# Squares of y: eight transposes a head replaced by 32x32 block turns and one small product

## What is computed

```
xn = layernorm(x)
q, k = rmsnorm(xn @ Wq), rmsnorm(xn @ Wk)          # per head of 128
attn = softmax(q k^T / sqrt(128) - slope * distance, causal)
y    = attn @ v                                    # 1024 x 128 per head
y    = y * rsqrt(mean(y*y over the 128 channels) + 1e-5) * subln_w
out  = x + concat(y) @ Wproj + ffn(xn)
```

## Time and profile before

| | |
|---|---|
| median of 3 runs | 545.61 us (545.49 to 545.79) |
| the profiled execution's own time | 543.86 us |
| its span, first to last instruction | 541.7 us |
| PE busy | 520.0 us (96%) |
| DVE, ACT, POOL busy | 414.7, 391.8, 334.3 us |
| granted TensorE clock | 1.00 of full speed throughout |

### The profile page before, as it was taken

How to read it: one execution, slowest core, us unless ns; L and a number is a source line. 1 busy time by engine, 2 the same in 40 slices (tenths; PEclk the granted TensorE clock), 3 DMA queues, 4 the chain that set the end, 5 groups by cost and what they waited for, 6 DMA issues and landing times.

```text
span 541.7 us, 11888 instructions
## 1 busy us (share of the span) xinstructions
PE 520.0 (96%) x3430; PEld 479.1 (88%) x3430; DVE 414.7 (77%) x1031; ACT 391.8 (72%) x887; POOL 334.3 (62%) x430
## 2 busy tenths in 40 slices
PE   7869899999999999999999999999999999999985
PEld 3868799999999999999999999999999999999874
DVE  5768778787788877877887877888778778868775
ACT  2668687686867778687777868778786876878662
POOL 4659575774758647684767748587476856647121
PEclk9999999999999999999999999999999999999999
DMA  5200101001010100101010010101001000000002
GB/s 150 69 1 2 40 0 41 2 1 41 2 39 0 39 0 0 39 0 39 0 39 0 0 39 0 39 0 31 8 0 39 0 10 0 11 1 1 2 1 79
DMA packets 18614, 10.83 MB, mean 20 GB/s; under 512 B 2208, under 2 KB 18592, under 8 KB 18592
## 3 DMA queue, kind: packets, MB, share of 16 engines
q1 hardware_dynamic: 17600, 10.49, 6.7%
q10 hardware_dynamic: 992, 0.07, 0.1%
HBM read 9.51 MB, written 1.05 MB: 19 GB/s over the span
## 4 chain that ended last, share of the span: by engine, by line
PE 87%; DVE 6%; ACT 3%; issue 2%; DMA 1%; POOL 1%; POOLq 0%; DVEq 0%; SPq 0%
PE pT_ps L564 11%; PE qkv_ps L479 10%; PE qkv_ps L481 8%; PE qkv_ps L480 8%; PE yT_ps L481 7%; PE yT_ps L480 7%; PE yT_ps L479 7%; PE score_big L479 5%; PE score_big L480 4%; PE score_big L481 4%; PE misc L540 3%; PE score_small L481 2%; PE score_small L480 2%; PE score_small L479 2%; ACT stage L743 2%
## 5 line engine op out<-in xcount | busy, mean ns | idle before, releaser
L934 DVE TENSOR_TENSOR pT_lo<-pT_ps,pT_hi 128x384 fp32r<-128x384 f32 (+1 forms) x192 | 101.0, 554 | 41.4 <-ACT pT_hi L771 41.2
L743 ACT ACTIVATE stage<-qkv_ps 128x384 f32<-128x384 f32 x119 | 58.7, 493 | 85.0 <-PE qkv_ps L481 84.5
L763 ACT ACTIVATE probs<-probs,neg_max 128x1024 f32<-128x1024 f32 (+7 forms) x128 | 98.5, 770 | 16.6 <-DVE neg_max L925 16.5
L771 ACT ACTIVATE pT_hi<-pT_ps 128x384 fp32r<-128x384 f32 (+1 forms) x192 | 86.3, 484 | 18.6 <-PE pT_ps L564 14.0
L432 POOL TENSOR_TENSOR y_r<-y_ms,minus_half 128x4 f32<-128x4 f32 x32 | 32.7, 1023 | 105.7 <-DVE y_ms L953 105.7
L479 PE MATMUL qkv_ps<-w_hi,xT_hi 128*128 128x384 f32 x242 | 87.2, 360 | 3.3 <-DVE xT_lo L994 0.7
L564 PE MATMUL pT_ps<-ident,probs 128*128 128x128 f32 x576 | 84.5, 274 | 4.2 <-ACT probs L763 3.5
L480 PE MATMUL qkv_ps<-w_lo,xT_hi 128*128 128x384 f32 x242 | 81.5, 337 | 0.0
L481 PE MATMUL qkv_ps<-w_hi,xT_lo 128*128 128x384 f32 x242 | 81.5, 337 | 0.0
L392 POOL TENSOR_TENSOR qk_r<-qk_ms,minus_half 128x4 f32<-128x4 f32 x64 | 65.5, 1024 | 20.9 <-DVE qk_ms L899 20.3
L564 PEld LDWEIGHTS pT_ps<-ident,probs 128*128 128x128 f32 x576 | 66.4, 140 | 9.2 <-ACT probs L763 4.4
(11 more groups left out here) (183 smaller groups left out, 1310.1 us busy)
## 6 DMA issues: line engine op xcount, KB each, us to landing
w_raw<-in_wq SPq DMA_DIRECT2D x16, 128.0 KB, 2.2
w_raw<-in_wk SPq DMA_DIRECT2D x16, 128.0 KB, 2.3
w_raw<-in_wv SPq DMA_DIRECT2D x16, 128.0 KB, 2.3
wp_raw<-in_wproj SPq DMA_DIRECT2D x16, 128.0 KB, 2.1
acc<-in_x SPq DMA_DIRECT2D x4, 256.0 KB, 4.8
out<-acc SPq DMA_DIRECT2D x8, 128.0 KB, 1.8
w<-in_ffn_w ACTq DMA_DIRECT2D x1, 64.0 KB, 5.2
q_col<-in_q_w ACTq DMA_DIRECT2D x1, 0.5 KB, 3.0
```

What stands on the lines that cost most here:

```text
L743: act.activation(stage_of(h, k // 2)[:, k % 2, :], qkv_bank(h, k)[:, 0:3 * D], ACT.Copy).then_inc(qkv_read, 1)
L763: act.activation(probs[:, s % 2, 0:(i + 1) * P], probs[:, s % 2, 0:(i + 1) * P], ACT.Exp, bias=neg_max[:, par, s:s + 1], scale=-1.0, accum ...
L771: act.activation(pT_hi[g][:, a:b, r * P:(r + 1) * P], pT_ps[(CHUNK0[s] + k) % 2][:, 0:(b - a) * P].rearrange("p (j t) -> p j t", t=P), ACT ...
L934: dve.tensor_tensor(pT_lo[g][:, a:b, r * P:(r + 1) * P], pT_ps[(CHUNK0[s] + k) % 2][:, 0:(b - a) * P].rearrange("p (j t) -> p j t", t=P), ...
```

## The change

The squares are taken on ACT straight from `yT_ps` (`square_y`, now in place of the copy to `y_raw`). DVE turns the 128x512 squares in blocks of 32x32 (`part_y`): after that a partition holds, for one token modulo 32, 32 channels of one quarter side by side, and a reduction over 32 gives `y_part`, 16 numbers per partition. Partition 32a+i then holds the sums over the channels of quarter a, for the tokens i of each block of 32. POOL splits `y_part` into hi and lo (`split_y`, two operations of 128x16), PE adds the four quarters by one product with the constant `quarters` (1/128 where the partitions agree modulo 32), 32 columns wide (`sum_y`). DVE masks with `in_quarter` which of four results belongs to the partition (`y_pick`) and reduces nine numbers per token tile, the eps term among them. `norm_y` and `add_out` stay. The two constants are made on DVE at the program's start.

Around it: `qkT0` moves from step 3 to step 4 and into the bank `yT`, so that `transpose_qk` 0 and 1 stand where one of them and a `turn_y` stood; ACT's `qk_hi` 0 and 1 both move, to the two sides of the last `copy_qkv` of step 4; DVE's mean of group 1 moves from step 5 to step 3; POOL's `split_y` of group 0 stands ahead of `split_w`.

```diff
-    MISC = ["ss0", "proj0a", "proj0b", "qkT0", "ss1", "qkT1", "qkT2", "qkT3", "proj1a", "proj1b"]
-    JOB_BANK = {"ss0": "qkv", "proj0b": "yT", "ss1": "yT", "qkT2": "qkv", "proj1a": "qkv"}
-    TAIL_BANK = {"ss0": "qkv", "proj0a": "small", "proj0b": None, "ss1": "big0", "proj1a": "qkv", "proj1b": "big1"}
+    MISC = ["proj0a", "proj0b", "qkT0", "qkT1", "qkT2", "qkT3", "proj1a", "proj1b"]
+    JOB_BANK = {"proj0b": "yT", "qkT0": "yT", "qkT2": "qkv", "proj1a": "qkv"}
...
+            def split_y(h, g):
+                pool.wait_ge(y_summed, 2 * h + g + 1)
+                past(pool, y_crossed, 2 * h + g)
+                pool.nop(nofuse=True)
+                part = y_part[:, :].rearrange("p (r c) -> p r c", c=4)
+                pool.tensor_copy(y_pair[:, :, 0, :], part).then_inc(y_part_hi, 1)
+                pool.wait_ge(y_part_hi, 2 * h + g + 1)
+                pool.nop(nofuse=True)
+                pool.tensor_tensor(y_pair[:, :, 1, :], part, y_pair[:, :, 0, :].bitcast(f32),
+                                   ALU.subtract).then_inc(y_paired, 1)
...
                 if tile is not None:
                     round_x(tile)
+                if not first:
+                    split_y(h - 1, 0)
...
                 if not (isinstance(h, int) and h + 2 >= H):
                     split_w(h + 2, par)
...
+                        if k == 0 and not first:
+                            split_y(h - 1, 1)
...
+                if job == "proj0a" and not tail:
+                    pe.wait_ge(y_picked, 2 * h - 1)
+                if job == "qkT1" or tail and bank == "qkv":
+                    past(pe, y_picked, 2 * h - 1 if tail else 2 * h)
...
-            def turn_y(h, g, now):
-                bank_free(now, f"ss{g}")
-                pe.wait_ge(y_copied, 2 * h + g + 1)
-                for r in range(4):
-                    last = pe.transpose(job_ps(h + 1, f"ss{g}")[:, r * P:(r + 1) * P], y_raw[:, g, r * P:(r + 1) * P],
-                                        ident[:, :])
-                last.then_inc(y_turned, 1)
+            def sum_y(h, g):
+                pe.wait_ge(y_paired, 2 * h + g + 1)
+                past(pe, y_picked, 2 * h + g)
+                if is_last(h) and g == 0:
+                    pe.wait_ge(misc_read, misc_done(h, "proj1a"))
+                elif is_last(h):
+                    pe.wait_ge(scores_masked, NT * H)
+                elif g == 0:
+                    pe.wait_ge(misc_read, misc_done(h, "qkT3" if isinstance(h, int) and h == 0 else "proj1b"))
+                else:
+                    pe.wait_ge(misc_read, misc_done(h + 1, "proj0a"))
+                if isinstance(h, int) and (h, g) == (0, 0):
+                    pe.wait_ge(w8T_read, 1)
+                pe.matmul(sum_ps(h, g), quarters[:, :], y_pair[:, :, :, :].rearrange("p r l c -> p (r l c)"),
+                          start=True, stop=True).then_inc(y_crossed, 1)
...
-                            turn_y(h - 1, 0, h)
                     if s == 1:
+                        if not first:
+                            sum_y(h - 1, 0)
...
-                        if s == 4 and not first:
-                            turn_y(h - 1, 1, h)
-                        elif not first:
+                        if s == 4 and not last:
+                            transpose_qk(h + 1, 1 - par, 0, h)
+                            transpose_qk(h + 1, 1 - par, 1, h)
+                        if s < 4 and not first:
                             if s == 3 and tile is not None:
                                 pe.wait_ge(ffn_added, tile + 1)
+                            if s == 3:
+                                sum_y(h - 1, 1)
                             project_out(h - 1, 1 - par, 0, s - 2, h)
                         if not last:
                             project(h + 1, 1 - par, 2 * s - 1)
-                    if s in (3, 4) and not last:
-                        transpose_qk(h + 1, 1 - par, s - 3, h)
...
-            turn_y(H - 1, 0, H)
             project_out(H - 1, 1, 0, 0, H)
+            sum_y(H - 1, 0)
             attend(H - 1, 1, 1, 0)
             attend(H - 1, 1, 1, 1)
             project_out(H - 1, 1, 0, 1, H)
-            turn_y(H - 1, 1, H)
+            sum_y(H - 1, 1)
...
-            def y_out(h, g):
+            def square_y(h, g):
                 act.wait_ge(yT_ready, 2 * h + g + 1)
-                act.activation(y_raw[:, g, :], yT_ps[:, :], ACT.Copy).then_inc(y_copied, 1)
+                past(act, y_turned, 2 * h + g - 1)
+                act.activation(y_sq[:, g, :], yT_ps[:, :], ACT.Square).then_inc(y_squared, 1)
+            def y_hi(h, g):
                 act.activation(yT_hi[:, g, :], yT_ps[:, :], ACT.Copy).then_inc(y_hi_done, 1)
-            def square_y(h, g):
-                act.wait_ge(y_turned, 2 * h + g + 1)
-                past(act, y_summed, 2 * h + g)
-                act.activation(y_sq[:, :], job_ps(h + 1, f"ss{g}"), ACT.Square).then_inc(y_squared, 1)
...
-                    if s == 1 and not first:
-                        square_y(h - 1, 0)
...
-                    if s == 4 and not last:
-                        qk_hi(h + 1, 1 - par, 0)
+                    if s == 2 and not first:
+                        square_y(h - 1, 1)
...
-                    if s == 4 and not first:
-                        square_y(h - 1, 1)
-                    if s == 5 and not last:
-                        qk_hi(h + 1, 1 - par, 1)
...
+                    if s == 4 and not last:
+                        qk_hi(h + 1, 1 - par, 1)
...
-                        y_out(h, 0)
+                        square_y(h, 0)
+                        y_hi(h, 0)
...
+            def part_y(h, g):
+                n = 2 * h + g
+                dve.wait_ge(y_squared, n + 1)
+                dve.transpose(y_blocks[:, :], y_sq[:, g, :]).then_inc(y_turned, 1)
+                dve.wait_ge(y_turned, n + 1)
+                past(dve, y_paired, n)
+                dve.nop(nofuse=True)
+                dve.tensor_reduce(y_part[:, :], y_blocks[:, :].rearrange("p (b j) -> p b j", j=32),
+                                  AX.X, ALU.add).then_inc(y_summed, 1)
             def y_mean(h, par, g):
-                dve.scalar_tensor_tensor(y_el2[:, g, :], row_sum[:, par, g, :], EPS, row_sum[:, par, g, :],
+                n = 2 * h + g
+                dve.scalar_tensor_tensor(y_pick[:, :, 8], row_sum[:, par, g, :], EPS, row_sum[:, par, g, :],
                                          ALU.mult, ALU.mult).then_inc(el2_ready, 1)
-                dve.wait_ge(y_squared, 2 * h + g + 1)
-                dve.tensor_reduce(y_ms[:, g, :], y_sq[:, :].rearrange("p (r d) -> p r d", d=D),
-                                  AX.X, ALU.add).then_inc(y_summed, 1)
-                dve.wait_ge(el2_ready, 2 * h + g + 1)
-                dve.wait_ge(y_summed, 2 * h + g + 1)
-                dve.scalar_tensor_tensor(y_ms[:, g, :], y_ms[:, g, :], 1.0 / D, y_el2[:, g, :],
-                                         ALU.mult, ALU.add).then_inc(y_meaned, 1)
+                dve.wait_ge(y_crossed, n + 1)
+                dve.tensor_tensor(y_pick[:, :, 0:8], sum_ps(h, g).rearrange("p (r n) -> p r n", n=8),
+                                  in_quarter[:, :, :].rearrange("p l c -> p (l c)").unsqueeze(1).broadcast_to([P, 4, 8]),
+                                  ALU.mult).then_inc(y_picked, 1)
+                dve.wait_ge(el2_ready, n + 1)
+                dve.wait_ge(y_picked, n + 1)
+                past(dve, y_normed, n - 1)
+                dve.nop(nofuse=True)
+                dve.tensor_reduce(y_ms[:, g, :], y_pick[:, :, :], AX.X, ALU.add).then_inc(y_meaned, 1)
...
+                dve.tensor_reduce(quarter_row[:, :], ident[:, :].rearrange("p (a i) -> p i a", i=32),
+                                  AX.X, ALU.add).then_inc(quarter_made, 1)
+                dve.tensor_reduce(in_quarter[:, 0, :], ident[:, :].rearrange("p (c i) -> p c i", i=32),
+                                  AX.X, ALU.add).then_inc(quarter_made, 1)
+                dve.wait_ge(quarter_made, 2)
+                dve.tensor_scalar(quarters[:, :].rearrange("p (c i) -> p c i", i=32),
+                                  quarter_row[:, :].unsqueeze(1).broadcast_to([P, 4, 32]), 1.0 / D, None, ALU.mult)
+                dve.tensor_copy(in_quarter[:, 1, :], in_quarter[:, 0, :]).then_inc(quarter_made, 1)
...
-                    if s in (4, 5) and not last:
-                        qk_lo(h + 1, 1 - par, s - 4)
+                    if s == 5 and not last:
+                        qk_lo(h + 1, 1 - par, 1)
...
+                    if s == 0 and not first:
+                        part_y(h - 1, 0)
+                    if s == 2 and not first:
+                        part_y(h - 1, 1)
+                    if s == 4 and not last:
+                        qk_lo(h + 1, 1 - par, 0)
...
-                    if s == 5 and not first:
-                        y_mean(h - 1, 1 - par, 1)
                     if s in (2, 3) and not first:
```

(6 more changed lines are left out.)

79 lines of the change are left out of this document (43 added, 36 removed).

## The result

The changed kernel takes **549.47 us** (median of 6 runs, 548.98 to 551.11) against 545.55 us of the kernel before (6 runs, 543.88 to 545.79), a ratio of 1.0088 with a 95% interval of 1.0074 to 1.0102 (the two medians by themselves give 1.0072; the times of the kernel before fall into two groups, see head 0 below). It is slower by 3.9 us where 1.1 us less was forecast; the value lies inside the range of 539.0 to 550.0 us. The profiled execution took 549.36 us, 547.6 of it span, so in spans the loss is 5.9 us (541.7 before).

The account below looks back on a forecast made before the run. PE's queue was taken to bound the middle, latency the tail. Gains of 6 x 0.66 + 8 x 0.26 = 6.0 us, less 0.4 in head 0 and 4.5 in the tail, net -1.1: 545.6 to 544.5 us, range 539.0 to 550.0.

Parts of the forecast that it names:

- the tail: After the last head's projections: longer waits and chain, +2.9 us before the last attend and +1.6 after, +4.5 us.
- head 0: First head: no y is turned, but the later qk_hi delays DVE's unbroken list, 0.4 us lost.
- What leaves and enters PE's queue: Per head, transposes and a stall of 1.18 us leave, two narrow products of 0.22 us enter.
- the two first parts: What leaves and what enters PE's queue: heads 1 to 14 gain 0.96 us each if nobody else is late.
- ACT at steps 4 and 5: Both qk_hi precede step 5's exponentials, so PE waits 0.30 us; a head without a tile gains 0.66 us.
- POOL in heads with a tile: Eight heads: split_y comes late, PE waits 0.33 us at sum_y; these heads gain 0.26 us each.
- cover just about used up: Step 2: the turn pushes DVE's y_lo to end at 295.85, when PE's FFN product wants it at 295.84.
- the terms of 2.9: Tail: the last attend starts at 532.4 instead of 529.46, +2.9 us; from its end on, +1.6 us.
- the load did come off PE: Denies the rival that a narrow product costs as much as four transposes, leaving no gain; no chance given.
- The waits do not come: Rival: ACT and POOL hand over 0.3 to 0.4 us sooner, middle heads gain up to 0.96 each, 537.1 us; chance 0.28.
- The wait of the second rival: Rival: DVE's turn takes 1.25 us, PE's FFN product waits 0.5 us for y_lo, 551.2 us in all; chance 0.13.
- my range: Whole kernel: 539.0 to 550.0 us for 8 in 10.

Follow-up runs that it names:

- tile_both: Changed kernel with sum_y of group 0 behind project 1 and, in tile heads only, group 1's turn and reduction behind yT_lo: 545.86 us, ratio 1.0011.
- el2_early: Changed kernel with DVE's four-column product of the row sums taken out of y_mean and issued at the start of step 0: 549.89 us, ratio 1.0094.
- tail_warm: Changed kernel with 11 and 13 idle products put ahead of the two sum_y of head 15: 547.34 us, ratio 1.0046.
- sum_twice: Changed kernel with each narrow product of sum_y issued twice into the same place: 551.92 us, ratio 1.0159.
- all_warm0: Changed kernel with the edits of tile_both and el2_early, qk_hi 1 behind step 5's exponentials, tail reordered, 8 idle products ending head 0: 532.59 us, ratio 0.9787.

## Why the prediction was wrong

Two steps of the sum failed: the tail, put at 4.5 us, and head 0, put at 0.4, were priced at an unchanged clock and measured 7.5 and 1.8; and in heads with a tile the turn at step 2 was priced at nothing, so that they lost 0.3 us in all instead of gaining 2.1.

**What leaves and enters PE's queue: right.** With these waits out of the way the heads take 30.96 and 30.57 us, 0.89 and 1.07 less than before, where the two first parts gave 0.96. The 0.11 for a narrow product measured 0.094.

**ACT at steps 4 and 5: right in place, its price too low.** A wait of 0.30 us ahead of the transposes of step 5 was forecast and is there; with the copy moved back the head gains 0.39 to 0.46, since a further wait followed. The copy itself keeps ACT 0.62 us (272.64 to 273.26) and not 0.73, since ACT's instructions overlap by up to 0.12 us here and not by less than 0.1. The heads without a tile gained 0.62 of the forecast 0.66, in part by luck: 0.11 more left PE's queue than forecast (1.07 for 0.96), and step 5 took 0.16 more (0.46 for 0.30).

**POOL in heads with a tile: right in its own term, wrong in what lies behind it.** The wait was 0.26 for 0.33. But the step that said of DVE "cover just about used up" priced the turn at step 2 at nothing in the sum, and it was 0.18 us of wait at the FFN product. With POOL's wait of 0.26 and what narrow products cost more after a wait, the two took 0.57 us a head (tile_both) where 0.33 stands in the sum. The rest of the difference of 0.35 a head is 0.07 from PE's queue (0.89 for 0.96) and 0.04 from step 5 (0.41 for 0.37). Also in that step: POOL's `w_lo` was moved 0.6 us later by `split_y` and I called it harmless because its result is needed a head later. It held up DVE's four columns by 1.4 us. That this cost nothing is shown by el2_early, but I did not know it when I called it covered, so that was luck. Forecast 8 x 0.26 gained, measured near 0.3 us lost in all.

**The tail: the term was mis-sized because it priced latency at an unchanged clock.** Of 7.5 us, 5.0 are the chain that I had walked at 4.5, and 2.5 are PE at half its clock after 2.93 us of standing. The sum had no term for it. In tail_warm, at full clock, the terms of 2.9 (ahead of `attend`) and 1.6 (from its end on) measure 3.2 and 1.8.

**Head 0: the same.** The forecast 0.4 is right where the clock stays up (27.19 us in sum_twice and 27.02 in all_warm0, against 26.81); the other 1.4 in the profile is a fall of the clock, which the kernel before shows too, in some executions.

**Rivals.** None of them happened as told. The turn took 0.704 us, POOL's small operations 0.42 together, and the load did come off PE. "The waits do not come" was the reverse of the case. The wait of the second rival, PE's FFN product for `y_lo`, did come, at 0.18 us instead of 0.5 and with a turn near the price I took. The larger part of the loss, the clock and the chain of the tail, was no mechanism in my list: -1.1 with +3.0 for the tail over its 4.5, +1.4 for head 0, +2.4 for the heads with a tile and +0.2 for the others gives +5.9, which are the 5.9 in spans. Of that the medians show 3.9, since the median of before, 545.55, contains the low clock in head 0, and its profile did not. That the value still lies inside my range is luck, since the range held no term for the clock.

## What to carry to other kernels

Put an operation that itself waits for others late in a full engine's queue, and not ahead of work whose operands are there: the operations saved gave 13.3 us in heads 1 to 14 only in the best order, and between that order and the change as made lie 15 us. Whether part of the same reordering would help the kernel before was not tested. When an edit makes TensorE stand for as long as here (1.8 to 2.9 us), count with what the products behind the wait cost at half the clock, or fill the wait with idle products. Waits in a row hide each other, so an edit that removes one and gains nothing may be right; remove the next before judging it.

## What was unexpected in the hardware

- The granted clock fell from 1.00 to 0.50 (2.4 to 1.2 GHz) in or soon after waits of TensorE of 1.92 us (kernel before, in one of four profiles), 2.2 us (nine of eleven), 1.83 us behind another of 1.69 (five of eleven) and 2.93 us (tail, in every profile with that wait), and a product of 512 columns then started 0.43 us after the one before instead of 0.23. In the changed kernel's tail it fell at 529.1 us, inside the wait that ended at 530.90. The same program takes 1.5 us more or less by it. The Trainium skill (TensorE: Matmul & The Clock Gate, section "Part 1: The HAM clock gate") says that the clock depends on how busy the array has been of late and that it has these two levels; the trace agrees. Which executions fall with the shorter waits is left open.
- Idle products in the wait kept the clock up: with 24 extra products (tail_warm) the program was 2.1 us faster.
- A DVE operation of four columns with both inputs in SBUF took 1.56 us beside a POOL pass of 1.84 us that had begun 0.30 us earlier, and 0.155 us without. It ended with that pass. The Trainium skill (SBUF — State Buffer, section "SBUF: two separate sides") describes such an exclusive hold of a shared port for a whole instruction; the trace agrees.
- A float32 turn of 128x512 in 32x32 blocks on DVE took 0.704 us, 0.02 more than a reduction of the same width.
